# A merged pipeline of attention, expert router and MLP: loads by need, keys before position biases, steps moved by a slot

## What is computed

```python
# block 1: attention-free transformer, local; x = layernorm(x), pos_encod = ctx
emb = x + pos_encod
q, k, v = emb @ wq + bq, emb @ wk + bk, emb @ wv + bv
w = pos_bias * (abs(i - j) < 64)
ek = exp(k - max(k, axis=1)); ew = exp(w - max(w, axis=1))
num = einsum('tj,bjd->btd', ew, ek * v); den = einsum('tj,bjd->btd', ew, ek)
attn = (sigmoid(q) * num / den) @ wo + bo
a = layer_norm(attn + emb); out = layer_norm(relu(a @ w1 + b1) @ w2 + b2 + a)
# block 2: router over 64 experts, top 8, x = layernorm(x)
probs = softmax(x @ router_w + router_b); tw, ti = top_k(probs, 8); tw /= sum(tw)
routed = sum over e of tw[e] * (silu(x @ w1[e] + b1[e]) @ w2[e] + b2[e])   # and two shared experts
```

## Time and profile before

| | |
|---|---|
| median of 3 runs | 1274.57 us (1273.88 to 1274.8) |
| the profiled execution: its own time | 1272.18 us |
| its span, first to last instruction | 1270.5 us |
| granted TensorE clock, mean | 0.979 |
| busy share PE, DVE, ACT, POOL | 90%, 69%, 55%, 27% |
| early phase (to the first product of the next) | 400.87 us |

### The profile page before, as it was taken

The page is one execution under the profiler, slowest core; times in us unless marked ns, Lnnn a source line. Parts: engine busy times, 40 slices in busy tenths (PEclk is TensorE's granted clock), DMA queues, the critical chain, the costliest instruction groups (busy, mean ns, idle before and its releaser), DMA issues. The chain is left out here.

```text
span 1270.5 us, 19924 instructions
## 1 busy us (share of the span) xinstructions
PE 1142.3 (90%) x6928; PEld 997.4 (79%) x6928; DVE 878.1 (69%) x1653; ACT 703.6 (55%) x1063; POOL 343.7 (27%) x343
## 2 busy tenths in 40 slices
PE   0778899788987999999999989999999999989998
PEld 0557788677877999999999978778788788777887
DVE  3576756766674655655755443999989989997575
ACT  1213323365543444444444233888988988986755
POOL 2520202251170510600600045512442442233120
PEclk9989999899998999999999999999999999998999
DMA  9200000004334444344332023321421423310001
GB/s 313 67 1 1 1 1 1 1 1 137 71 71 112 113 115 138 94 120 134 91 95 54 1 76 100 100 58 59 136 64 54 138 62 119 95 39 5 14 24 48
DMA packets 68967, 92.88 MB, mean 73 GB/s; under 512 B 16016, under 2 KB 33168, under 8 KB 68752
## 3 DMA queue, kind: packets, MB, share of 16 engines
q1 hardware_dynamic: 67264, 89.67, 25.0%
q10 hardware_dynamic: 1616, 2.10, 0.5%
HBM read 80.45 MB, written 11.14 MB: 72 GB/s over the span
## 5 line engine op out<-in xcount | busy, mean ns | idle before, releaser
L1997 DVE CUSTOM_DVE_ANT_0 at_pr<-at_sc,at_mk 128x512 f32<-128x512 f32 x256 | 165.5, 683 | 26.2 <-PE at_sc L2228 25.7
L1901 ACT ACTIVATE at_pr<-at_pr,at_nmx 128x512 f32<-128x512 f32 x256 | 170.5, 717 | 17.8 <-DVE at_nmx L1997 17.2
L2139 DVE TENSOR_TENSOR W_1l<-at_pt,W_1h 128x1024 fp32r<-128x1024 f32 x128 | 155.8, 1218 | 6.1 <-ACT W_1h L1896 5.7
L1896 ACT ACTIVATE W_1h<-at_pt 128x1024 fp32r<-128x1024 f32 x128 | 130.8, 1022 | 34.7 <-PE at_o L2262 33.2
L2243 PE MATMUL at_pt<-ident,at_pr 128*128 128x128 f32 x1024 | 135.2, 275 | 15.0 <-DVE W_1l L2139 14.2
L2243 PEld LDWEIGHTS at_pt<-ident,at_pr 128*128 128x128 f32 x1024 | 115.3, 142 | 38.4 <-issue 17.0
L228 ACT ACTIVATE moe_hs<-moe_hid,cols 128x512 f32<-128x512 f32 x120 | 82.8, 690 | 100.4 <-PE moe_hid L114 99.5
L247 DVE TENSOR_TENSOR moe_hl<-moe_ms,moe_hh 128x512 fp32r<-128x512 f32 x104 | 80.4, 773 | 64.3 <-ACT moe_hh L220 64.3
L261 DVE TENSOR_TENSOR moe_ms<-moe_hs,gate 128x512 f32<-128x512 f32 x104 | 78.7, 757 | 57.4 <-ACT moe_hs L228 57.0
L220 ACT ACTIVATE moe_hh<-moe_ms 128x512 fp32r<-128x512 f32 x104 | 65.8, 633 | 94.2 <-DVE moe_ms L261 94.2
L2262 PE MATMUL at_o<-W_1h,at_vaug 128*128 128x512 f32 x256 | 112.1, 438 | 0.3 <-DVE W_1l L2139 0.3
(11 more groups left out here) (304 smaller groups left out, 3304.2 us busy)
## 6 DMA issues: line engine op xcount, KB each, us to landing
gate<-expert_weights SPq DMA_DIRECT2D x256, 128.0 KB, 3.0
w_stage<-in_ew SPq DMA_DIRECT2D x32, 256.0 KB, 4.0
at_kp<-at_heads SPq DMA_DIRECT2D x96, 64.0 KB, 2.7
at_qp<-at_heads SPq DMA_DIRECT2D x96, 64.0 KB, 2.8
w_stage<-in_mask SPq DMA_DIRECT2D x16, 256.0 KB, 3.6
at_rb<-at_recip SPq DMA_DIRECT2D x64, 64.0 KB, 2.1
w_stage<-in_w SPq DMA_DIRECT2D x8, 256.0 KB, 7.3
w_stage<-in_sw SPq DMA_DIRECT2D x8, 256.0 KB, 3.3
```

What stands on the lines that cost most here:

```text
L1896: act.activation(PH[0][:, n % 2, :], PT[n % 2][:, :, :].rearrange("p c q -> p (c q)"), ACT.Copy)\
L1901: act.activation(pr_of(t)[:, x, :], pr_of(t)[:, x, :], ACT.Exp, bias=nmx[:, t % 4, x:x + 1], scale=-1.0).then_inc(s["ex"], 1)
L1997: dve.tensor_tensor_reduce(pr_of(t)[:, x, :], SB[x][:, :], mk[u // 2 % 2][:, j, :], -float(HD) ** -0.5, 3.0e38, ALU.add, ALU.min, nmx[:, t ...
L2139: dve.tensor_tensor(PH[1][:, n % 2, :], PT[n % 2][:, :, :].rearrange("p c q -> p (c q)"), f(PH[0][:, n % 2, :]), ALU.subtract).then_inc(s[ ...
```

## The change

Seven edits, all in `early_phase`:
1. **Loads.** The ACT queue loads the four weights ahead of the position biases; the SP queue loads `ident` ahead of `cols`. Each has a semaphore of its own, so that the start of the prologue doesn't wait for the large `rows` any more.
2. **Prologue.** The split of the projection weights is cut in four, in the order of use. `key(0)` and `value(0)` stand ahead of the turning of the position biases (`turn_ew`), which is interleaved with `query(0)`. `turn_ek(1)`, `denominators(1)`, `ek_low(1)`, `den_times(1)`, `emb_stats(2)` and `emb_apply(2)` stand in the prologue, not in pass 0. The keys of batch 1 use other banks for it (`key_banks`).
3. **`emb_apply` is cut in two**: the addition of the output bias is `emb_bias`, which stands later.
4. **Attention steps** of batch `turned` stand one slot sooner on all engines: `denominators` slot 0 (was 1), `turn_ekv` 1 (2), `numerators` 2 (3); `turn_ek` slot 7 of the pass before. `project_out`, `z_stats`, `z_scaled` and `turn_z` stay in slots 4 to 7.
5. **Projections** of batch `early`: `key` slot 3 (was 2), `value` 5 (4), `query` 7 (6); `emb_apply` slot 7 of the pass before (was 0), `emb_stats` 4 (7 of the pass before).
6. **Router** steps one slot sooner: `turn` slot 7 of the pass before, `logits` 1 (2), `turn_logits` 2 (3), `choose` 2 (3), `exponentials` 3 (4), `normalise` 4 (5). `turn_weights`, `weights` and `biases` stay in 6 and 7, as do `stats`, `centre` and `new_x` in theirs, and `add_y` in 2.
7. **POOL**: `add_beta` of two batches waits for the numerators of a batch and stands in a loop with `root_emb`, `root_z`, `add_b2`.

The core of the diff:

```diff
+            sp.dma_start(g.ident[:, :], a["ident"]).then_inc(af["id"], 16)
+            sp.dma_start(g.cols[:, :], a["cols"]).then_inc(af["cols"], 16)
...
+            for b in range(B - 1):
+                if b:
+                    pool.wait_ge(af["num"], 2 * b + 2)
+                    for k in (2 * b - 2, 2 * b - 1):
+                        add_beta(k)
+                if b + 2 < B:
+                    root_emb(b + 2)
+                root_z(b)
+                add_b2(b)
...
-            act.dma_start(pos[:, :, :], a["pos"].rearrange("(t p) n -> p t n", p=P)).then_inc(af["pos"], 16)
             for j, n in enumerate(("wq0", "wk0", "wv0", "wo0")):
                 act.dma_start(wst[:, j], a[n].rearrange("(c p) n -> p c n", p=P)).then_inc(af["w"], 16)
+            act.dma_start(pos[:, :, :], a["pos"].rearrange("(t p) n -> p t n", p=P)).then_inc(af["pos"], 16)
             act.wait_ge(af["w"], 64)
-            act.activation(W[0][:, :, :, :], wst, ACT.Copy).then_inc(af["wh"], 1)
+            for j in (1, 2, 0, 3):
...
-                        if t == 1:
+                        if t == 0 and i:
                             ek_high(turned)
-                        if t == 3:
+                        if t == 2:
                             ekv_high(turned)
                         if t == 7:
                             z_high(turned)
+                    if early < B and t == 4:
+                        exp_k(early)
                     if n < LAST:
                         relu(n)
...
-                    if turned < B and t == 4:
+                    if early < B and t == 1:
+                        emb_high(early)
+                    if turned < B and t == 3:
                         y_high(turned)
-                    if early < B and t == 6:
+                    if early < B and t == 7:
                         exp_q(early)
                     if i == B - 1 and t < 4:
                         if t == 0:
@@ -803,11 +810,11 @@
                         high_group1(2 * t + 1)
                     if t == 0 and i >= 3:
                         turn_high(i - 3)
-                    if t == 2 and i >= 3:
+                    if t == 1 and i >= 3:
                         logits(i - 3)
                     if t == 3 and 2 <= i <= B + 1:
                         centre(i - 2, 0, attn_of(i - 2), xh, s["sh1"], s["new"], 1, s["xh"])
-                    if t == 4 and i >= 3:
+                    if t == 3 and i >= 3:
                         exponentials(i - 3)
...
+            def emb_bias(b):
                 dve.wait_ge(af["et"], b + 1)
                 dve.tensor_tensor(attn_of(b), emb[:, :, :], tiles(g.row("bo0"), TT), ALU.add).then_inc(af["ab"], 1)
...
+                dve.wait_ge(af["ab"], min(b + 2, B))
...
-            dve.wait_ge(g.consts, 48)
             emb_apply(0)
+            for k, j in enumerate((1, 2, 0, 3)):
+                dve.wait_ge(af["wh"], k + 1)
+                dve.tensor_tensor(W[1][:, j, :, :], wst[:, j], f(W[0][:, j, :, :]), ALU.subtract).then_inc(af["wl"], 1)
+            emb_low(0)
+            dve.wait_ge(af["cols"], 16)
             dve.tensor_scalar(nbq[:, :], g.cols[:, col_at("bq0"):col_at("bq0") + C], -1.0, None, ALU.mult)\
                .then_inc(af["nbq"], 1)
+            dve.wait_ge(af["band"], 2)
+            dve.tensor_reduce(npm[:, :], pos[:, :, :], AX.X, ALU.max, negate=True).then_inc(af["npm"], 1)
+            dve.wait_ge(af["nbq"], 1)
+            k_max(0)
+            weighted(0)
+            ew_low(0)
+            ew_low(1)
             dve.wait_ge(af["rest"], 32)
             emb_stats(1)
-            dve.wait_ge(af["nbq"], 1)
-            dve.wait_ge(af["band"], 2)
-            dve.tensor_reduce(npm[:, :], pos[:, :, :], AX.X, ALU.max, negate=True).then_inc(af["npm"], 1)
-            dve.wait_ge(af["wh"], 1)
-            dve.tensor_tensor(W[1][:, :, :, :], wst, f(W[0][:, :, :, :]), ALU.subtract).then_inc(af["wl"], 1)
-            emb_low(0)
+            ew_low(2)
+            ew_low(3)
+            dve.wait_ge(g.consts, 16)
+            emb_bias(0)
             emb_apply(1)
-            for jc in range(TT):
-                dve.wait_ge(af["ewh"], jc + 1)
-                dve.tensor_tensor(ewT[1][:, jc, :], YB[jc % 2][:, :], f(ewT[0][:, jc, :]), ALU.subtract).then_inc(af["ewl"], 1)
-            k_max(0)
-            weighted(0)
             ek_low(0)
             emb_low(1)
             den_times(0)
+            emb_bias(1)
             invert(0, 0)
             ekv_low(0)
             k_max(1)
             invert(0, 1)
+            emb_stats(2)
             make_y(0)
             y_low(0)
+            z_stats(0)
             weighted(1)
-            z_stats(0)
-            emb_stats(2)
+            ek_low(1)
             z_scaled(0)
+            den_times(1)
+            z_low(0)
+            emb_apply(2)
...
-                        if t == 1:
+                        if t == 0 and i:
                             ek_low(turned)
+                        if t == 1 and i:
+                            den_times(turned)
                         if t == 2:
-                            den_times(turned)
+                            ekv_low(turned)
                         if t == 3:
-                            ekv_low(turned)
-                        if t == 4:
                             make_y(turned)
                         if t == 5:
                             z_stats(turned)
@@ -1081,33 +1103,35 @@
                     if i == B + EARLY:
                         continue
                     if turned < B:
-                        if t in (2, 3):
-                            invert(turned, t - 2)
-                        if t == 4:
+                        if t in (1, 2):
+                            invert(turned, t - 1)
+                        if t == 3:
                             y_low(turned)
                         if t == 6:
                             z_scaled(turned)
                     if early < B:
-                        if t == 0:
-                            emb_apply(early)
                         if t == 1:
                             emb_low(early)
-                        if t == 2:
+                        if t == 3:
                             k_max(early)
                         if t == 4:
+                            emb_bias(early)
+                            if early + 1 < B:
+                                emb_stats(early + 1)
+                        if t == 5:
                             weighted(early)
                         if t == 7 and early + 1 < B:
-                            emb_stats(early + 1)
-                    if t == 1 and i >= 3:
+                            emb_apply(early + 1)
+                    if t == 0 and i >= 3:
                         turn_low(i - 3)
                     if t == 2 and 2 <= i <= B + 1:
                         stats(i - 2, 0, attn_of(i - 2), s["yadd"], 2 * (i - 2) + 2, s["bn1"], s["mv1"])
-                    if t == 3 and i >= 3:
+                    if t == 2 and i >= 3:
...
+                    if t == 4 and i >= 3:
                         normalise(i - 3)
 
         @block.tensor
...
+            pe.wait_ge(af["id"], 16)
+            turn_emb(0)
             key(0)
             value(0)
+            turn_ew(0)
+            turn_ew(1)
             query(0)
+            turn_ew(2)
+            turn_ew(3)
             turn_ek(0)
             turn_emb(1)
             denominators(0)
@@ -1284,8 +1319,10 @@
             turn_ekv(0)
             value(1)
             numerators(0)
+            query(1)
             project_out(0)
-            query(1)
+            turn_ek(1)
+            denominators(1)
             turn_z(0)
             for i in range(B + EARLY + 1):
                 turned, early = i + 1, i + 2
@@ -1296,18 +1333,16 @@
                     if early < B:
                         if t == 1:
                             turn_emb(early)
-                        if t == 2:
+                        if t == 3:
                             key(early)
-                        if t == 4:
+                        if t == 5:
                             value(early)
-                        if t == 6:
+                        if t == 7:
                             query(early)
                     if 3 <= i < B + EARLY:
-                        if t == 0:
-                            turn(i - 3)
+                        if t == 1:
+                            logits(i - 3)
                         if t == 2:
-                            logits(i - 3)
-                        if t == 3:
                             turn_logits(i - 3)
                         if t == 6:
                             turn_weights(i - 3)
@@ -1316,18 +1351,20 @@
                     if 2 <= n < LAST + 2:
                         output(n - 2)
                     if turned < B:
-                        if t == 0:
-                            turn_ek(turned)
+                        if t == 0 and i:
```

(17 more changed lines are left out.)

78 lines of the change are left out of this document (36 added, 42 removed).

## The result

Before 1274.12 us (median of 19 runs, 1269.26 to 1277.79), after 1277.48 (19 runs, 1275.41 to 1280.65): ratio 1.0027, 95% interval 1.0016 to 1.0037. The change makes the kernel 0.27% slower. I had forecast 1270.2 and faster; only the range, 1260 to 1281, holds. Ratios are of fast runs alone; two slow ones, 1335 and 4170 us in e3, are in none. The profiled execution took 1276.94 us, its span 1275.1, with a mean clock of 0.965 (before 0.979).

The account below looks back on a forecast made before the run. In each pass the DVE or ACT result that PE waits for was taken to decide. The terms −10.9 −5.2 +2.3 +0.9 +1.2 +5.3 +5.3 −3.3 summed to −4.4 us, from a 1274.6 median to 1270.2; range 1260 to 1281.

Parts of the forecast that it names:

- prologue: Start to first hidden product: `denominators(0)` at 41.0 instead of 56.3, first hidden product at 81.4 against 92.3, 10.9 us gained.
- pass 1: Attention: new wait of 4.5 us for `add_y`, 3.9 at `turn_z`, clock behind both; 59.5 against 57.2, 2.3 us lost.
- pass 2: Attention: waits of 4.2 at `add_y`, 3.2 at an output, 3.5 at `turn_z`, 2.9 for clock; 0.9 us lost.
- pass 5: Router: early exponentials with table loads delay `new_x` and gating weights, late gate loads add 0.5; 39.7 against 34.4, 5.3 lost.
- pass 6: Router without `centre` and `new_x`: `normalise` ready at 25 instead of 26.8, `biases` doesn't wait; 3.3 us gained.
- Rival A: Passes 3 to 5: the router's move is free, their 11.8 us of waits fall away, 1258.4 us; chance 0.18.
- I charge 1.7 us behind a long wait: PE behind a long wait: half clock for 3.4 us, so 1.7 us charged unless a later wait absorbs it.
- dense prices: PE times from windows without waits: 2.72 us a projection, 1.36 a hidden product, 1.43 a tile's output product.
- `logits`, a slot sooner, waits 1.8 us for `turn_low`: Router, passes 3 to 6: PE's wait for the low part of the router's turned input, 1.8 us.
- a stretch at half clock goes: Pass 6: PE's half-clock stretch disappears, one part of the 3.3 us gained there.
- Rival B: Passes 0 to 2: head start eaten, new waits delay the next projections, 10 us in all, 1280.2; chance 0.20.
- C: Whole kernel: it cancels, 11 us gained ahead of pass 0 and 11 lost behind, within 2.5 of 1274.6; chance 0.24.

Follow-up runs that it names:

- e3: Changed kernel with `add_y` of passes 1 and 2 moved on DVE to slot 1, ahead of the reciprocal; 1270.91 us, ratio 0.9967 to the kernel before.
- e1: Changed kernel with all router steps back in the slots of the kernel before; 1266.0 us, ratio 0.9939 to the kernel before.
- e6: e5 with 24 needless transposes on PE ahead of each `turn_weights`; 1253.6 us, ratio 0.9842 to the kernel before.
- e11: Kernel before, with only 24 needless transposes on PE added ahead of each `turn_weights`; 1270.7 us, ratio 0.9965 to the kernel before.
- e8: Changed kernel with `weights` ahead of the second `centre` in slot 6 on ACT; 1273.04 us, ratio 0.9997 to the kernel before.
- e4: Kernel before with only the new loads, prologue order and cut `emb_apply`, without the moved steps of batches 1 and 2; 1262.95 us, ratio 0.9906.
- e5: Changed kernel with e1 and e3 together: router steps back, `add_y` a slot sooner in passes 1 and 2; 1260.14 us, ratio 0.9879.
- e10: Changed kernel with `turn` and `turn_low` still a slot sooner, all other router steps back in their old slots; 1262.57 us, ratio 0.989.
- e2: Changed kernel with only `exponentials` and `normalise` back in slots 4 and 5; 1273.54 us, ratio 0.9993 to the kernel before.

## Why the prediction was wrong

Step by step, what I forecast for the profiled execution and what it showed, in us (minus is gained):

| | forecast | measured |
|---|---|---|
| prologue | -10.9 | -9.3 |
| pass 0 | -5.2 | -3.8 |
| pass 1 | +2.3 | +3.7 |
| pass 2 | +0.9 | +2.6 |
| pass 3 | +1.2 | +1.4 |
| pass 4 | +5.3 | +4.8 |
| pass 5 | +5.3 | +8.0 |
| pass 6 | -3.3 | -0.5 |
| behind the early phase | 0 | -2.2 |
| sum (before rounding) | -4.4 | +4.8 |

Two sums of the prediction don't come out as written. The terms of its pass 2 make 52.5 us; the 53.5 need the 1.0 of `turn`, which edit 6 moves into the end of that pass. And its passes charge 2.5, 3.4 and 2.9 us for the clock, 8.8 together, where its sum speaks of 7.1.

**Right.** `denominators(0)` started at 41.05 us (41.0 forecast). PE waited 4.3 and 4.0 us for `add_y` (4.5 and 4.2), 3.8, 3.9 and 3.2 for `turn_z` (3.9, 3.9, 3.5), 3.1 at `numerators(1)` (3.2). The gating weights of pass 4 started 30.7 us in (30.7), those of pass 5 at 33.1, 2.4 later than forecast. The exponentials stand with both table loads behind `centre`, here in pass 4 (start, duration, line, operation):

```profile
302.71 2.08 ACT L717 ACTIVATE rt_xh<-attn,rt_shift,rt_rstd 128x256 f32<-128x256 f32 x4 [1.31 <-POOL rt_shift L572]
304.80 1.28 ACT L736 ACT_TABLE_LOAD   x1
306.10 1.07 ACT L736 ACTIVATE rt_ex<-rt_lg,rt_ntop 128x64 f32<-128x64 f32 x4
307.18 1.28 ACT L653 ACT_TABLE_LOAD   x1
308.48 0.69 ACT L653 ACTIVATE f_hs<-f_hid,cols 128x512 f32<-128x512 f32 x1
...
318.26 0.69 ACT L653 ACTIVATE f_hs<-f_hid,cols 128x512 f32<-128x512 f32 x1 [6.47 <-DVE f_hl L831]
...
321.33 0.36 ACT L742 ACTIVATE rt_cwo<-rt_r 128x256 f32<-128x256 f32 x1
```

From the end of `centre` at 304.79 to the activation are 3.7 us, the price taken from the earlier trace rows. The two loads take 1.28 us each, with 1.07 of exponentials between them. By the Trainium skill (ScalarE: Activation LUTs, What ACT_TABLE_LOAD costs) a drain of 1.38 us should stand with each load; the trace shows none here either. The last two rows show what the step cost: the activation of slot 6 waits 6.5 us for a low part, and `weights` follows it and the second `centre`. Rival A, the router's move is free, is refuted by e1: undone, it gives 11.5 us back, where I had summed 8.5.

**The step that failed** is the size of two terms, and both come back, in the main, to the clock behind a wait. First, *"I charge 1.7 us behind a long wait"*, which made 8.8 us in passes 0 to 2, and nothing elsewhere. In these three passes PE stood idle for 24.9 us, where the waits of the forecast make 26.4. But it was busy for 141.6, where the dense prices make 126.7 (with the 1.0 of `turn`): 14.9 us over dense, and 8.8 were charged. 6.0 too little there and 1.5 too much in the waits are the 4.5 us by which these passes were longer than forecast. By the clock column, 0.93, 0.92 and 0.85, up to 16.7 us can be lost to half clock in them (one minus the clock, times the length; an estimate). The kernel before held the warning: it was busy there for 142.3 us against 134.1 of dense prices, 8.1 over. In the prologue I charged nothing, and `denominators(1)` stands behind a new wait of 4.85 us:

```profile
72.39 0.79 PE L114 MATMUL rt_r<-W_1h,aft_kTh 128*128 128x512 f32 x1 [4.85 <-DVE aft_kTl L970]
...
77.58 0.39 PE L114 MATMUL rt_r<-W_1h,aft_kTh 128*128 128x512 f32 x1
```

Its matmuls are 0.43 us apart up to 77.25 and 0.23 from the second row on; it took 7.9 us, where the 5.5 of dense ones would have made the first hidden product come at 80.6 and not 83.0 (an estimate). That is the 1.6 us by which the prologue fell short, and more. The same wait of 4.85 us, with half clock behind it, stands in all eleven profiled executions with this prologue. That the clock is what a wait costs beside its own length, e6 and e11 show.

Second, *"`logits`, a slot sooner, waits 1.8 us for `turn_low`"*. In pass 3 it waited 1.42, in pass 4 1.73. In pass 5:

```profile
328.71 0.69 DVE L838 TENSOR_TENSOR f_hs<-f_hs,gate 128x512 f32<-128x512 f32 x1 [3.51 <-DMA gate<-expert_weights]
...
329.92 1.28 DVE L909 TENSOR_TENSOR x_res<-rt_r,x_res 128x512 f32<-128x512 f32 x2
...
331.12 1.28 DVE L872 TENSOR_TENSOR xT_l<-rt_r,xT_h 128x512 fp32r<-128x512 f32 x2
...
332.50 0.47 PE L114 MATMUL rt_r<-xT_h,rt_rwh 128*128 128x512 f32 x1 [2.56 <-DVE xT_l L872]
```

the gate product (L838) waits for its gate until 328.71, 0.9 us after the activation it also needs was there, and `turn_low` (L872) stands behind it on DVE: 2.56. The gates hang on SP's queue behind the store of the late weights, whose issues in pass 4 were at

```profile
321.72 1.28 SPq L557 DMA_DIRECT2D expert_weights<-rt_cwo  x2
324.52 5.65 SPq L547 DMA_DIRECT2D gate<-expert_weights  x8
```

and I had given this 0.5. In pass 6 it is another cause, DVE,

```profile
370.25 1.11 DVE L838 TENSOR_TENSOR f_hs<-f_hs,gate 128x512 f32<-128x512 f32 x1 [1.83 <-ACT f_hs L653]
371.28 1.77 DVE L831 TENSOR_TENSOR f_hl<-f_hs,f_hh 128x512 fp32r<-128x512 f32 x1
...
374.18 1.27 DVE L872 TENSOR_TENSOR xT_l<-rt_r,xT_h 128x512 fp32r<-128x512 f32 x2
```

beside POOL, which splits MLP weights without a pause:

```profile
370.89 1.61 POOL L411 TENSOR_TENSOR W_0l<-w_stage,W_0h 128x512 fp32r<-128x512 f32 x1
```

The gate product takes 1.11 us for 0.69 and the low part 1.77 for 0.68, each against its time in pass 4: 1.5 us more, 1.73 becomes 3.24. In before DVE ran as slowly in this place (0.84 and 1.78 ahead of `turn_low`), but `logits` was a slot away. And behind both waits PE ran on at half clock, with the router's chain in it (same columns as above):

```profile
332.50:336.93 4.43, 4.43 (x19) 4.04 (x20) 1.10 (x2) 0.69 (x1) 0.00 (x0) 0.61 1.00 139
375.55:382.41 6.86, 6.86 (x24) 5.91 (x25) 3.48 (x4) 0.69 (x1) 6.62 (x7) 0.58 0.24 56
```

The first stretch takes 4.4 us for 2.9 dense ones (the like in e3: 2.90 at clock 1.00), and the next steps, `turn_logits`, `choose`, `exponentials`, `new_x`, come 1.5 later. With the 0.3 by which the wait of 2.56 is above the forecast's 1.8 and 0.5 that is 1.8 of the 2.7 by which pass 5 was longer than forecast; the other 0.9 was not traced. The pass of e3, with the same code, a wait of 1.81 and no such stretch, took 39.3 us (39.7 forecast). In pass 6 the wait is 1.4 more than forecast, and its stretch at half clock costs 2.6 (`logits`, output and hidden product 2.70, 2.56 and 1.60 us by the distance of the starts, against 1.46, 1.44 and 1.39 at full clock in e8), partly covered later: e8's pass 6, behind the same wait, was 1.6 shorter. I had written that in pass 6 *"a stretch at half clock goes"*. It moved to another wait.

**Rival B** had its mechanism (`add_y` behind `ekv_low`, `numerators` behind it), and e3 shows 6.6 us for it (7.1 without its two long runs); but its point of decision, a loss of 5 us in passes 0 to 2, was not reached: they lost 2.5. **C**, it cancels, came nearest as a mechanism: the head start of 9.3 was lost behind. The measured time is 3.4 us above that of the kernel before, 0.9 outside C's 2.5, so by the time alone it is B's "slower", well short of B's price. The cause in one line: edit 6 costs 11.5 us, the place of `add_y` 6.6, and the prologue, worth 11.4 alone, pays for part of it. Of the -2.2 us behind the early phase no run shows a cause; it is within what this part varied by (867.2 to 870.7 us).

**Open.** Edit 7 was not tried by itself. How the loss divides between edits 4, 5 and 7 and the steps of batches 1 and 2 in the prologue is known only as a sum: e1, which has them, takes 3.1 us more than e4, which doesn't; with `add_y` mended (e5) it is 2.8 less.

## What to carry to other kernels

When a hand-made pipeline is moved a slot sooner, count for each step the distance in slots to what it needs, on every engine. Here a producer moved sooner cost nothing (`turn`, e10), while the consumer moved along with it stood nearer to it and waited, with everything queued behind it (`logits`, e2). A step that stays in its slot can lose as well, when steps that moved now stand ahead of it in its engine's list (`add_y`, e3). Price each wait of the tensor engine twice, its length and the slower clock of what follows, and where the wait can't be removed, try work that nobody needs in it. Reread the table of waits after each mend: three orders of a few DVE instructions were worth 5.5, 7.7 and 9.8 us in the passes in which they stand (6.6, 8.8 and 11.9 by medians). And compare the stages in which an edit stands before adding medians up: the same prologue varied by 2.8 us from trace to trace.

## What was not expected of the hardware

- PE's clock behind a wait isn't a fixed price. `logits` in pass 6 waited 3.24 us in both the changed kernel and e8, and ran on at 0.58 (above) in the one and at full clock in the other:

```profile
371.89:375.04 3.15, 3.15 (x20) 2.84 (x21) 2.15 (x3) 0.69 (x1) 3.07 (x3) 1.00 0.12 44
```

  `numerators` waited 2.1 us in pass 1 of e4 and of e11, and the next product started 7.2 us later in the one and 5.6 in the other. So one profile can show 1.6 us of it, or none, at the same wait, and medians are needed.
- Needless transposes in a wait of PE made the kernel faster each time, by 6.5, 3.6 and 2.2 us by medians, for 96 instructions; passes 3 to 6, in which they stand, took 140.9 us each time, against 145.1, 144.6 and 148.1 without them.
- A DVE subtraction of 128x512 (`f_hl`) took 0.68 us, and 1.77 beside POOL's subtraction of 128x512 (rows at 371.28 and 370.89 above).
